# Statistics and streamed units placed anew, and the last and first tiles of a band cut to what they hold

## What is computed

```python
def _gn(v, G=8, eps=1e-5): ...                      # mean and variance over 2 channels x 2048 x 2048

causal_mask = tril(ones(H, W))
xm = where(causal_mask, _gn(x), 0)
y  = conv(xm, weight[:, None], 6 x 11 taps, one filter per channel, padding (5,0),(5,5))
x  = x + where(causal_mask, y, 0)                   # layer 0

table = relu(relu(pos @ W1 + b1) @ W2 + b2) @ W3 + b3     # pos = -(n-1) .. n-1
x  = x + (_gn(x) + table[i - j])                    # layer 1: x * (1 + 1/s) - m/s + bias
```

## Time and profile before

| | us |
|---|---|
| median of 3 runs | 2638.41 (2633.20 to 2640.93) |
| profiled execution | 2638.45 |
| its span | 2636.7 |
| DVE busy | 2304.3 (87%) |
| PE busy | 1979.8 (75%) |
| ACT busy | 1660.3 (63%) |
| POOL busy | 1260.7 (48%) |
| moved by DMA | 894.88 MB, mean 339 GB/s |

### The profile page before, as it was taken

One profiled execution on the slowest core, in us unless ns is written; L12 is line 12 of the kernel. 1 busy time (PEld: TensorE's weight loads), 2 busy tenths in 40 slices (PEclk: granted clock), 3 DMA queues, 4 the chain that ended last, 5 costly groups with the idle time before them and its releaser, 6 DMA issues. The chain is left out here.

```text
span 2636.7 us, 76763 instructions
## 1 busy us (share of the span) xinstructions
PE 1979.8 (75%) x28880; PEld 1876.5 (71%) x28880; DVE 2304.3 (87%) x4175; ACT 1660.3 (63%) x3051; POOL 1260.7 (48%) x1988
## 2 busy tenths in 40 slices
PE   4289988888687876878778877888868778899800
PEld 0289887878687776877778776787768778899800
DVE  7799988899888997899888998889988899778846
ACT  2167766766576675766667666666656757687722
POOL 1123235535545454454555445554554546475543
PEclk9999998999899999999898999999889998999955
DMA  9775649999899998999989998999989997797999
GB/s 337 273 243 170 233 136 384 393 371 351 329 408 377 380 337 332 402 359 385 354 334 396 359 366 329 378 392 362 348 329 395 384 373 297 284 355 274 334 370 360
DMA packets 313546, 894.88 MB, mean 339 GB/s; under 512 B 42272, under 2 KB 42272, under 8 KB 311296
## 3 DMA queue, kind: packets, MB, share of 16 engines
q1 hardware_dynamic: 198528, 576.64, 59.3%
q10 hardware_dynamic: 114832, 316.22, 31.0%
HBM read 576.36 MB, written 316.53 MB: 339 GB/s over the span
## 5 line engine op out<-in xcount | busy, mean ns | idle before, releaser
L1184 PEld LDWEIGHTS psY<-wsplit,XT 128*128 128x128 f16 x25920 | 1607.2, 102 | 355.9 <-DVE XT L801 128.6
L1184 PE MATMUL psY<-wsplit,XT 128*128 128x168 f16 (+5 forms) x25920 | 1635.9, 223 | 290.7 <-DVE XT L801 240.2
L659 ACT CAST XT<-psT 128x512 f16<-128x512 f32 x720 | 414.8, 576 | 561.0 <-PE psT L1170 325.5
L1110 POOL COPY halo<-XT 128x16 f16<-128x16 f16 x720 | 318.9, 443 | 657.5 <-DVE XT L801 647.3
L801 DVE TENSOR_TENSOR XT<-psT,XT 128x512 f16<-128x512 f32 x720 | 493.8, 686 | 140.3 <-ACT XT L659 139.4
L1084 POOL TENSOR_TENSOR xn<-xn,mask 128x512 f32<-128x512 f32 x336 | 423.7, 1261 | 387.5 <-ACT xn L647 325.8
L829 DVE BATCH_NORM_STATS2 entries<-ring 128x6 f32<-128x512 f32 x872 | 551.4, 679 | 61.3 <-DMA ring<-in_x 61.0
L1170 PE MATMUL psT<-ident,xn 128*128 128x128 f32 x2880 | 480.3, 292 | 98.2 <-POOL xn L1084 77.6
L1119 POOL TENSOR_TENSOR ring<-ring,bias 128x1024 f32<-128x1024 f32 x181 | 408.4, 2258 | 253.7 <-ACT ring L708 253.6
L647 ACT ACTIVATE xn<-kept_c_band,normp 128x512 f32<-128x512 f32 (+2 forms) x496 | 398.4, 803 | 48.3 <-DMA kept_c_band<-in_x 26.9
L1170 PEld LDWEIGHTS psT<-ident,xn 128*128 128x128 f32 x2880 | 317.8, 146 | 107.4 <-POOL xn L1084 72.5
(11 more groups left out here) (81 smaller groups left out, 486.2 us busy)
## 6 DMA issues: line engine op xcount, KB each, us to landing
ring<-in_x SPq DMA_DIRECT2D x628, 512.0 KB, 8.6
out<-ring ACTq DMA_DIRECT2D x282, 512.0 KB, 6.1
kept_c_band<-in_x SPq DMA_DIRECT2D x224, 512.0 KB, 8.1
out<-kept_c_band ACTq DMA_DIRECT2D x224, 512.0 KB, 7.0
band<-in_x SPq DMA_DIRECT2D x48, 1024.0 KB, 11.3
out<-band ACTq DMA_DIRECT2D x45, 1024.0 KB, 8.7
ring<-out SPq DMA_DIRECT2D x90, 512.0 KB, 9.5
bias<-bias_scratch SPq DMA_DIRECT2D x16, 1793.5 KB, 8.5
```

What stands on the lines that cost most here:

```text
L659: nc.scalar.copy(XT[:, n % NB3, 0, :, 2:P + 2], psT[n % NB3][:, :, :]).then_inc(hi_ready, 1)
L1110: nc.gpsimd.tensor_copy(halo[:, t, :, :, :], XT[:, n % NB3, :, :, P:P + 2]).then_inc(halo_out, 1)
L1184: last = nc.tensor.matmul(psY[m][:, 0:rows, o + lo_c:o + hi_c], XT[:, m, xp, i, 2 - sh:2 - sh + P], wsplit[:, c, wp, K * sh:K * sh + rows, ...
```

## The change

Four things change.

1. `book` puts a kept block's store at `kept_pos + 3` instead of `+ 1` and its reload at `reload_pos + 2` instead of `+ 0`. The kept blocks themselves stay where they were; only the units that are placed around them move.
2. `U_WEIGHT` gets 2.2 instead of 1.8 below place 10, 1.8 instead of 1.0 at 47 to 54, 1.2 instead of 1.5 above 82.
3. `n_pieces` counts how many of a tile's 4 pieces hold data. It is 2 for tiles 4, 44, 49 and 89, 3 for tiles 13 and 58, else 4. `split_hi`, `split_lo`, `halo_to`, `mask_tile`, `transpose` and `convolve` work on that many. PE's loops over triples of tiles can then stand only where all tiles have 4 pieces: of 30 triples a group, 16 stay in loops where 25 did, the other 14 are written out (5 before).
4. `left_of_diag` counts the columns of a tile left of the diagonal block, where the mask is 1. The mask multiplications skip them on DVE (tiles 9, 22 and 39 of each channel: 332, 172 and 12 elements of 472) and, by whole pieces, on POOL.

```diff
+    n_pieces = [-(-min(TIN, BW * (b + 1) - STEP * t) // XC) for c, b, t in TILES]
+    left_of_diag = [max(0, BW * b - STEP * t) for c, b, t in TILES]
...
-    U_WEIGHT = lambda n: 1.8 if n < 10 else 1.5 if n > 82 else 1.0
+    U_WEIGHT = lambda n: 2.2 if n < 10 else 1.8 if 46 < n < 55 else 1.2 if n > 82 else 1.0
...
             if do_c:
-                book(kept_pos[blk][0] + 1, 1.0)
+                book(kept_pos[blk][0] + 3, 1.0)
             if do_b:
-                book(reload_pos(blk, 0), 1.0)
+                book(reload_pos(blk, 0) + 2, 1.0)
...
-                nc.vector.tensor_tensor(XT[:, n % NB3, 1, :, 2:P + 2], psT[n % NB3][:, :, :],
-                                        XT[:, n % NB3, 0, :, 2:P + 2], ALU.subtract).then_inc(lo_ready, 1)
+                np = n_pieces[n]
+                nc.vector.tensor_tensor(XT[:, n % NB3, 1, 0:np, 2:P + 2], psT[n % NB3][:, 0:np, :],
+                                        XT[:, n % NB3, 0, 0:np, 2:P + 2], ALU.subtract).then_inc(lo_ready, 1)
...
-                    nc.vector.tensor_tensor(y, y, mask_at(b, t, c0, c1), ALU.mult).then_inc(conv_masked, 1)
+                    d0 = max(c0, left_of_diag[n])
+                    y_diag = psY[n % NB3][:, :, d0:c1]
+                    nc.vector.tensor_tensor(y_diag, y_diag, mask_at(b, t, d0, c1), ALU.mult).then_inc(conv_masked, 1)
...
-                v = xn[:, n % NB3, :, :, :]
+                i0, i1 = left_of_diag[n] // XC, n_pieces[n]
+                v = xn[:, n % NB3, i0:i1, :, :]
...
-            def transpose(N, m):
+            def transpose(N, m, np=NPC):
...
-                products = [(i, sh, xp, wp) for i in range(NPC) for sh in range(3)
+                products = [(i, sh, xp, wp) for i in range(np) for sh in range(3)
...
+            def looped(j):
+
+                return all(n_pieces[(NB3 * j + i) % NT] == NPC for i in range(NB3 + 2))
+
+            def triples(first, c, lo, hi):
+
+                while lo < hi:
+                    end = lo
+                    while end < hi and looped(end):
+                        end += 1
+                    if end - lo > 1:
+                        with pe.Fori(lo, end) as j:
+                            triple(first + NB3 * j, c)
+                    else:
+                        end = lo + 1
+                        triple(first + NB3 * lo, c, first=NB3 * lo)
+                    lo = end
```

More of the change, by code:

```diff
@@ L1188, in convolve, with triple @@
                 last.then_inc(convolved, 1)
-            def triple(N, c, ahead=NB3, results_of=None):
+            def triple(N, c, ahead=NB3, results_of=None, first=None):
+                pieces = [NPC if first is None else n_pieces[(first + i) % NT] for i in range(NB3 + 2)]
                 for i in range(NB3):
                     if i < ahead:
-                        transpose(N + i + 2, (i + 2) % NB3)
+                        transpose(N + i + 2, (i + 2) % NB3, pieces[i + 2])
                     if i == 0 and results_of is not None:
                         sum_results(results_of)
-                    convolve(N + i, i, c)
+                    convolve(N + i, i, c, pieces[i])
+            def looped(j):
[12 more added lines that the diff above has]
+                    lo = end
             def sum_means(g):
@@ L1215, in group @@
                 pe.wait_ge(w_built, chan(g, 0) + 1)
-                triple(first, 0, results_of=g - 1 if before else None)
-                with pe.Fori(1, NTC // NB3) as j:
-                    triple(first + NB3 * j, 0)
+                triple(first, 0, results_of=g - 1 if before else None, first=0)
+                triples(first, 0, 1, NTC // NB3)
                 pe.wait_ge(w_built, chan(g, 1) + 1)
-                triple(first + NTC, 1)
-                with pe.Fori(NTC // NB3 + 1, SUM1[0] if after else 2 * NTC // NB3 - 1) as j:
-                    triple(first + NB3 * j, 1)
+                triples(first, 1, NTC // NB3, SUM1[0] if after else 2 * NTC // NB3 - 1)
                 if after:
-                    triple(first + NB3 * SUM1[0], 1)
+                    triples(first, 1, SUM1[0], SUM1[0] + 1)
                     sum_means(g + 1)
-                    triple(first + NB3 * SUM1[1], 1)
+                    triples(first, 1, SUM1[1], SUM1[1] + 1)
                     sum_variances(g + 1)
-                    with pe.Fori(SUM1[1] + 1, 2 * NTC // NB3 - 1) as j:
-                        triple(first + NB3 * j, 1)
+                    triples(first, 1, SUM1[1] + 1, 2 * NTC // NB3 - 1)
             sum_means(0)
```

20 lines of the change are left out of this document (11 added, 9 removed).

## The result

The changed kernel takes 2700.02 us (median of 4 runs, 2695.53 to 2706.84) against 2638.33 for the kernel before beside it: ratio 1.0238, interval 1.0211 to 1.0266. It is slower by 2.4%, and far outside the predicted range. The profiled execution, the fastest of the four (2695.53), has a span of 2693.7 us, 57.0 more than before. Cut at the same evictions as before (L824 now), 46.9 of the 57.0 us lie in the six laps, 7.8 a lap; 2.6 in stage 1 and ahead of it, 0.3 in stage 8, 7.2 in the tail.

A forecast was written before the change was run, and what follows sets the result against it. No single bound: DVE limits some stretches, full DMA queues others, a serial chain behind DVE the lap's end. Terms sum to -0.9 us a lap, -5.4 over six, with 5 from narrow tiles -10.4: 2638.45 to 2628.0 us, range 2600 to 2655.

The forecast's parts named there:

- +6 at place 8: ACT at place 8 waits 6 us for a ring load whose buffer must first be stored (10.6 us store, 9.2 load).
- -5.1 + 1.1 at places 13 to 15 and -1.0: Statistics-load wait of 5.12 us at place 13 shrinks to about 1 to 2; -1.0 is slower catching up recovered.
- 10 us at place 8: Upper bound of +5 for places 1 to 15: wait of 10 at place 8, matmuls after it once at 3.64.
- Ports: Rival: DVE's two-input work and POOL's additions collide; 46 to 50 becomes +0.2, total 2638, chance 0.20. Forecast itself counted +1.5.
- -3.9 at 46 to 50: Places 46 to 50: four statistics units leave, one u comes on DVE, -3.9 us with the narrow tiles.
- the kept reloads come no sooner: Places 56 to 60: two statistics units leave (-2.5), but with share 1.05 and reloads no sooner, only -1.0 counted for 56 to 75.
- Narrow tiles: Stages 1 and 8, where PE is partly on the path: 5 us faster together, bounds 1 and 12.
- the rival that priced them at -6: PE's code: fewer loop passes bring at most -6 us of issue waits, sum 2622; no separate chance given.
- keeps its bytes, and I count it at 0, within 4: Tail, share 0.95: same bytes, so no change, within 4 us either way.
- the quick queue: Rival: place 8's load lands in time, lap -6.3 us, total 2595; chance 0.20.
- The slower one: Rival: turnaround at place 8 waits in full, at ACT's place 8 and DVE's 9; +5, total 2652, chance 0.20.
- signs of being wrong: No ring-load wait before place 15 (gain nearer 40 us), L991 mean above 1.6 us, PE issue waits well above 17 us.

The follow-up runs named there:

- the near cut: Changed kernel, the 14 streamed units at places 3 to 9 and 47 to 53 load and store only 16 of 128 partitions: 2610.97 us, 0.9916.
- weight 1.4: Kernel before with the narrow tiles and U_WEIGHT below place 10 at 1.4 instead of 1.8: 2675.36 us, 1.0158.
- reloads first: Changed kernel, SP issues kept blocks' reloads ahead of streamed units' loads at each place: 2680.98 us, 1.0174 to the kernel before.
- the small additions: Changed kernel, POOL's bias additions for units at places 3 to 9 and 47 to 53 cut to an eighth of the columns: 2671.14 us, 1.0143.
- weight 1.4 and 1.0: Two kernels: the kernel before with narrow tiles and that weight below place 10 instead of 1.8; 2675.36 us (1.4) and 2652.35 us (1.0).

## Why the prediction was wrong, point by point

The prediction gave -0.9 us a lap; it was +7.8. By its own cuts, in means of six laps:

| places | predicted | measured |
|---|---|---|
| 1 to 15 | +1.0 (-4.4 to +5) | +5.0 |
| 16 to 40 | -2.5 (-5 to 0) | -4.8 |
| 41 to 55 | -1.5 (-3.0 to +1.0) | +3.5 |
| 56 to 75 | -1.0 (-1.6 to 0) | +4.8 |
| 76 to 85 | +1.0 (0 to 1.9) | -2.5 |
| 86 to lap end | +2.1 (2.1 to 2.4) | +1.8 |

**What bounds the kernel: the first step that failed.** The prediction noted a share of 0.98 over 300 us of a lap and then argued from stretches of five places, as if a stretch where "the queues have room" gave time for nothing. The room was not free: units put there made their stores, the ring loads that wait for them and the kept reloads come in one bunch behind it, and the store and the reload that a norm waits for took 13.9 and 12.0 us instead of 10.9 and 6.9. The prediction has no term for transfers that get slower for others. In the account of the DMA engines it shows as 7.0 us more idle time in a lap, though by the near cut and weight 1.4 the length of a lap doesn't follow that idle time.

**Places 1 to 15: the wait at place 8 didn't come, another one did.** The term was +6 at place 8, -5.1 + 1.1 at places 13 to 15 and -1.0. The step that failed is the +6: a store of 10.6 us and a load of 9.2 were carried over from the earlier trace rows to a stretch where the queues are half empty. There the store took 3.7 us and the load behind it 4.0, nearly as quick as the earlier trace rows; neither ACT's L713 at place 8 nor DVE's L1010 at 9 waits in any of the six laps. The statistics load at 13 is no longer waited for, as forecast: DVE's idle time for such loads at places 11 to 15 fell from 4.5 us to nothing. But 6.3 us of waiting for ACT (1.1 before) came in its place, behind the norm of place 14. The two kept reloads were named as queued, and nobody asked who reads reloads. So places 11 to 15 came out at +0.3 where some -4 was expected; reloads first gave 3.8 of it. The rest of the +5.0 is +1.9 at places 1 to 5, where the ports explain it, and +2.9 at 6 to 10. These 2.9 are open: DVE idles 3.0 us there where it idled 0.5, for PE and for ACT, and reloads first (0.1 more), the near cut (-0.2) and the small additions (-0.6) all leave most of it. That the sum is just the upper bound of +5 is luck. The bound itself was 10 us at place 8 (10 - 5.1 + 1.1 - 1.0 = +5.0); the slow matmuls that it names are not in that sum.

**Ports: mechanism right, size off.** The prediction priced them at +1.5 at places 46 to 50 and at nothing at 1 to 5; the mean rose by 0.67 and 0.59 us on five instructions each, and cutting the additions brought 2.8 us back in each stretch. That is why the statistics units that left (-3.9 at 46 to 50) gave 0.6. As a rival it was 2638; it alone explains about 40% of the loss (25 us). The rule of the Trainium skill that stood beside it (page "SBUF — State Buffer", section "SBUF: two separate sides": an exclusive lock, the later one blocks fully) agrees with the row of 2.49 us against a 2.35 us addition, and with the tail, where it is POOL that was blocked.

**Places 16 to 55: moved, not gained.** 26 to 40 fell by 7.6 us, more than forecast. But 41 to 45 rose by 4.3, with DVE idle 3.43 us for the load of the unit at 41 in the lap shown, and 56 to 60 by 4.0. The kernels with weight 1.4 and 1.0 show the same pair, -4.1 at 36 to 40 and over +3 at 41 to 45. That transfers bind here is argued from the share (1.03 at 41 to 45); no run changes this stretch alone.

**Places 56 to 75** had "the kept reloads come no sooner" as a reason for a small number; they came later, and the norm at 59 waits 10.94 us. Its reload was issued at 1544.13, 5.5 us into the stretch, where before it went out 0.6 us ahead of it: the store of its half took 10.7 us instead of 5.4, and SP was busy issuing for 2.5 more. A ring load that DVE needs at the same time stands behind it and landed at 1556.16 (the wait of 7.42 us). Cutting the near transfers takes 5.9 us off 56 to 60 but adds 3.1 at 61 to 65; reordering SP does nothing.

**76 to 85** gained. DVE's work there didn't grow by 1.9 us, as forecast, but fell by 1.0: of its finishing instructions for streamed units four stand there as before, yet they take 1.4 us instead of 2.1 in the mean. Its idle time fell by 1.4. **The lap's end** came as predicted: 29.60 us in the lap shown (forecast about 29), +1.8 in the mean.

**Narrow tiles**: 5 us, of which 1.4 came alone, inside the bounds and not to be told from nothing. Together with them PE's written-out triples bring no difference; the rival that priced them at -6 is neither shown nor excluded. Waits for issue at the convolution grew from 17.3 to 31.1 us.

**Tail**: "keeps its bytes, and I count it at 0, within 4": +7.2. Bytes were the wrong view again; the order of DVE's and POOL's work on them changed, and the DMA share fell from 0.96 to 0.89.

Of the rivals, the quick queue had the facts of place 8 right and the time wrong by 100 us. The slower one had the place wrong, since nothing at 8 and 9 waits for the turnaround of the ring; that its +5 for places 1 to 15 is what was measured is luck. Two of the signs of being wrong came, no wait on ring loads before place 15 and waits for issue well above 17 us, but the first was read as a gain of 40 us; L991's mean (L999 now) stayed at 1.58, just under its 1.6, since it mixes these places with all others.

## What to carry to other kernels

A stretch in which the DMA queues idle is not a free reserve where they are full nearly everywhere else (here 0.65 in one stretch, 0.96 over the lap). Before moving work into it, write down what the DMA engines will do in it, whether the loads that could fill it wait for stores, and what the bunch that comes behind it does to the transfers that someone waits for. Follow every reload from the store that frees its place to its reader, however many places on, and price that wait by the times of a full queue; price a turnaround in the idle stretch by the times of an idle one. Don't take a shorter sum of idle time for a shorter lap. And don't put two-input work of GpSimd beside two-input work of VectorE in a stretch that VectorE sets.
